# Two macaron half-steps around an attention block: tile 13's rows of the second half turned by transposing DMA, and the written-out order laid out anew

## The reference, cut to what matters

```
def ffn(x):                                   # 128 -> 512 -> 512 -> 512 -> 128, exact gelu
    h = silu(x @ w1.T * w1_s) * (x @ w2.T * w2_s)
    h = gelu(h @ h1.T * h1_s)
    h = gelu(h @ h2.T * h2_s)
    return h @ w3.T * w3_s

def attention(x):                             # per sequence of 256 tokens, no softmax matrix
    h = layer_norm(x) * gamma + beta
    keys, values = h @ Wk.T + bk, h @ Wv.T + bv
    w = exp((keys @ Wka.T + bka) / sqrt(128))
    w = w / cumsum(w, axis=1)
    return cumsum(w * keys, axis=1) * values

x = x + 0.5 * ffn(layernorm(x))               # x is 16 sequences x 256 tokens x 128 features
x = x + attention(layernorm(x))
x = x + 0.5 * ffn(layernorm(x))
```

## Time and profile before

| | |
|---|---|
| runs, median of 3 | 367.9 us (365.8 to 368.27) |
| the profiled execution's own time | 367.03 us |
| its span | 365.2 us |
| PE busy | 356.0 us, 97% |
| DVE busy | 309.7 us, 85% |
| ACT busy | 291.9 us, 80% |
| POOL busy | 174.5 us, 48% |
| granted TensorE clock | 1.0 |
| mean DMA rate | 67 GB/s |

### The profile page before, as it was taken

The page is one execution under the profiler, slowest core; times in us unless marked ns, Lnnn a source line. Parts: engine busy times, 40 slices in busy tenths (PEclk is TensorE's granted clock), DMA queues, the critical chain, the costliest instruction groups (busy, mean ns, idle before and its releaser), DMA issues.

```text
span 365.2 us, 5048 instructions
## 1 busy us (share of the span) xinstructions
PE 356.0 (97%) x1524; PEld 276.7 (76%) x1524; DVE 309.7 (85%) x542; ACT 291.9 (80%) x475; POOL 174.5 (48%) x271
## 2 busy tenths in 40 slices
PE   6899999999999999999999999999999999999996
PEld 1678888878777677887777778788778777868885
DVE  4989877898999989988998988998889899685733
ACT  4798777997997899779979888978876985757763
POOL 3476247388178398656556537352364342210000
PEclk9999999999999999999999999999999999999999
DMA  7725505134006003502113008030030030600001
GB/s 248 252 86 168 173 2 115 29 78 110 17 4 163 9 0 63 173 0 64 55 58 88 1 0 144 2 116 1 2 106 11 4 85 0 173 3 29 1 2 59
DMA packets 30206, 24.58 MB, mean 67 GB/s; under 512 B 20065, under 2 KB 21345, under 8 KB 29921
## 3 DMA queue, kind: packets, MB, share of 16 engines
q1 hardware_dynamic: 29312, 23.30, 23.8%
q10 hardware_dynamic: 864, 0.93, 0.8%
HBM read 18.89 MB, written 2.19 MB: 58 GB/s over the span
## 4 chain that ended last, share of the span: by engine, by line
PE 85%; ACT 4%; DVE 3%; DMA 3%; issue 2%; POOL 1%; POOLq 0%; SPq 0%; DVEq 0%; ACTq 0%
PE hid_ps L724 56%; PE y_ps L724 7%; PE gate_ps L724 7%; PE up_ps L724 6%; PE xt_ps L920 2%; PE xt_ps L917 2%; PE xt_ps L913 2%; DMA wide<-rows 1%; DMA raw_w<-w1t 1%; PE gate_ps L788 1%; ACT hid_ps L983 1%; DVE act_lo L1184 1%; PE up_ps L788 1%; DVE gate L1162 1%; ACT tanh L964 1%
## 5 line engine op out<-in xcount | busy, mean ns | idle before, releaser
L724 PE MATMUL hid_ps<-act_hi,hi_h 128*128 128x512 f32 (+1 forms) x368 | 148.4, 404 | 0.4 <-DVE act_lo L1184 0.4
L724 PE MATMUL hid_ps<-act_lo,hi_h 128*128 128x512 f32 (+1 forms) x368 | 143.4, 390 | 0.0
L983 ACT ACTIVATE hid_ps<-hid_ps,vec 128x512 f32<-128x512 f32 x104 | 68.5, 661 | 43.5 <-PE hid_ps L724 42.7
L1184 DVE TENSOR_TENSOR act_lo<-hid_ps,act_hi 128x512 fp32r<-128x512 f32 x104 | 70.0, 681 | 23.7 <-ACT act_hi L990 23.0
L724 PEld LDWEIGHTS hid_ps<-act_hi,hi_h 128*128 128x128 f32 x368 | 69.1, 188 | 21.4 <-DVE act_lo L1184 6.2
L724 PEld LDWEIGHTS hid_ps<-act_lo,hi_h 128*128 128x128 f32 x368 | 69.1, 188 | 16.9 <-issue 2.4
L990 ACT ACTIVATE act_hi<-hid_ps 128x512 fp32r<-128x512 f32 x104 | 61.3, 599 | 2.2
L1184 DVE TENSOR_TENSOR act_lo<-full,act_hi 128x512 fp32r<-128x512 f32 x53 | 38.7, 739 | 15.3 <-ACT act_hi L990 14.7
L724 PE MATMUL hid_ps<-act_hi_second,hi_h 128*128 128x512 f32 x128 | 51.4, 401 | 0.0
L724 PE MATMUL hid_ps<-act_lo_second,hi_h 128*128 128x512 f32 x128 | 50.0, 390 | 0.0
L641 POOL TENSOR_TENSOR xnt<-xt_sb,wide 128x512 f32<-128x512 f32 x22 | 28.8, 1307 | 39.1 <-DMA wide<-rows 31.0
(11 more groups left out here) (173 smaller groups left out, 598.5 us busy)
## 6 DMA issues: line engine op xcount, KB each, us to landing
wide<-rows SPq DMA_DIRECT2D x44, 256.0 KB, 3.9
out<-xt_sb SPq DMA_DIRECT2D x7, 256.0 KB, 4.2
raw_h<-h2t SPq DMA_DIRECT2D x4, 256.0 KB, 6.5
x_sb<-x SPq DMA_DIRECT2D x1, 1024.0 KB, 5.0
xt_sb<-xt SPq DMA_DIRECT2D x1, 1024.0 KB, 5.0
x_sb<-x SPq DMA_DIRECT2D x3, 256.0 KB, 3.5
raw_h<-h1t SPq DMA_DIRECT2D x2, 256.0 KB, 5.7
xt_sb<-xt SPq DMA_DIRECT2D x2, 256.0 KB, 4.1
```

What stands on the lines that cost most here:

```text
L724: mm = eng.matmul(ps, w, a, start=(first and n == 0), stop=(last and n == len(seq_) - 1))
L983: eng.activation(gelu_out(n, T, m)[:, :], home23(n, T, m)[:, :], ACT.Gelu, scale=col("sh1" if n == 2 else "sh2", m)).then_inc(s_gelu[n], 1)
L1184: eng.tensor_tensor(act_lo[a][:, m, :], full[:, :], act_hi[a][:, m, :].bitcast(F32), ALU.subtract).then_inc(s_lo[n], 1)
```

## The change

The tuple `BY_DMA` gets `("ffn", 13)`. The list of PE loses `13:u`; POOL gets `13:split`, SP `13:turn`, ACT `13:join`. Apart from these four items every engine's list holds the same items as before, in an order laid out anew. The parts of it that the prediction speaks of:

- Opening: ACT examines w2 before it converts w1; DVE takes tile 1's statistics after `low1.0` instead of between `gate.0` and `gate.1`; ACT does `tanh.2` after `high1.0` and `high1.1`.
- SP: `a7:turn` moves from directly behind `a6:turn` to behind the new `13:turn`, `8:store` and `9:store`; `10:store` ahead of `a7:park`, `11:store` ahead of `15:park`. Before, `9:store`, `10:store` and `11:store` stood between `15:park` and `15:wide`.
- POOL: `a7:split` moves from behind `a6:split` to behind the new `13:split`, which follows `a5:dt`.
- ACT: `a7:join` moves from behind `10:high2.2` to behind the new `13:join`, which stands between `11:high2.0` and `11:gelu2.1`.
- PE: `10:p4` moves from ahead of `11:p2.0` to behind `11:p2.1`; `12:p1.2` takes its place. DVE: `a5:pool` and `a5:values` move ahead of `11:low1.2`, `11:low1.3`, `10:low3.1` and `12:gate.0`.
- SP: `a6:turn` directly behind `12:turn`, ahead of `11:wide`; ACT: `a6:join` directly behind `12:join`.

```diff
 START
-        "hi:w1 bits:w2 hi:w2 z 0:t vec:s1",
-        "tanh.0 tanh.1 bits:h1.1 bits:h1.3 tanh.2 high1.0 high1.1 bits:h2.0 tanh.3 bits:w3 high1.2 z.0 z.1 "
+        "bits:w2 hi:w1 hi:w2 z 0:t vec:s1 0:tanh.0 0:tanh.1 bits:h1.1 bits:h1.3",
+        "high1.0 high1.1 tanh.2 tanh.3 bits:h2.0 bits:w3 high1.2 z.0 z.1 high1.3 bits:h2.3 1:t 0:gelu2.0 "
...
-        "stats aggr veps bits:w1 norm.0 norm.1 flag:copy1 norm.2 bits:h1.0 0:t bits:h1.2 vec:scales",
-        "gate.0 stats gate.1 up.0 flag:raise2 up.1 flag:copy2 low1.0 aggr gate.2 veps up.2 gate.3 bits:h2.1 "
+        "stats aggr veps bits:w1 norm.0 flag:copy1 norm.1 norm.2 bits:h1.0",
+        "t bits:h1.2 vec:scales gate.0 gate.1 up.0 flag:raise2 up.1 flag:copy2 low1.0 stats gate.2 aggr veps "
...
 STEPS, SP
-        "11:wide a6:turn a7:turn 12:park a6:park",
-        "12:wide a6:wide",
-        "",
-        "13:park a7:park 13:wide a7:wide",
-        "",
-        "park wide 8:store 15:park",
-        "9:store 10:store 11:store wide store",
+        "12:turn a6:turn 11:wide 12:park 12:wide a6:park a6:wide",
+        "13:turn 8:store 9:store a7:turn 13:park",
+        "",
+        "10:store a7:park",
+        "wide a7:wide 14:park 14:wide 11:store 15:park 15:wide",
...
+        "12:store 13:store store",
 STEPS, POOL
-        "10:xn.1 a5:xn.0 a5:xn.1 norm a4:weight a4:dt 12:split a6:split a7:split",
+        "a4:weight a4:dt 12:split a6:split",
+        "xn.0 xn.1 12:norm a6:norm a5:weight",
+        "xn.0 xn.1 a6:xn.0 a6:xn.1 a5:dt 13:split a7:split 13:norm a7:norm",
 STEPS, PE
-        "9:p4 10:p2.3 a5:values 10:p3.0 10:p3.1 12:p1.0 12:p1.1 10:p3.2 10:p3.3 a6:logits 10:p4 11:p2.0 13:u "
-        "11:p2.1 12:p1.2 11:p2.2 12:p1.3 11:p2.3 a6:keys",
+        "12:p1.0 12:p1.1 10:p3.2 10:p3.3 a6:logits 12:p1.2 11:p2.0 11:p2.1 10:p4 11:p2.2 12:p1.3 11:p2.3 "
+        "a6:keys",
 STEPS, ACT
+        "10:high3.3 a6:logits gelu2.0 high2.0 join a7:join gelu2.1 high2.1 gelu2.2 high2.2 tanh.2 high1.0 "
...
-BY_DMA = (("att", 1), ... ("ffn", 11), ("ffn", 12))
+BY_DMA = (("att", 1), ... ("ffn", 11), ("ffn", 12), ("ffn", 13))
```

More of the change, by code:

```diff
@@ L53 @@
     "SP": (
-        "park wide 3:park 3:wide a0:park a0:wide 4:park 4:wide a1:turn a1:park 5:park a1:wide 5:wide 6:park",
-        "",
-        "6:wide a2:turn a2:park 7:park a3:turn",
[12 rows of a table added]
         "",
@@ L59 @@
         "",
-        "a2:wide 7:wide turn 9:turn a3:park park a4:turn a3:wide wide 9:park 9:wide 10:turn a5:turn a4:park "
-        "a4:wide 10:park a5:park 10:wide 11:turn a5:wide 11:park 12:turn",
-        "11:wide a6:turn a7:turn 12:park a6:park",
-        "12:wide a6:wide",
-        "",
-        "13:park a7:park 13:wide a7:wide",
-        "",
-        "park wide 8:store 15:park",
-        "9:store 10:store 11:store wide store",
-        "store",
-        "store",
[1 row of a table added]
     ),
     "POOL": (
-        "norm hi:h2.0 hi:h2.1 hi:h2.2 hi:h2.3 hi:w3 xn.0 xn.1",
-        "",
[L75 to L78, removed]
[14 rows of a table added]
         "",
-        "split a4:split 8:norm a2:weight norm a3:xn.0 a3:xn.1 8:xn.0 8:xn.1 xn.0 a2:dt",
[1 row of a table added]
         "",
-        "10:split a5:split a4:norm 9:xn.1 a4:xn.0 10:norm a3:weight a4:xn.1 a5:norm a3:dt split 10:xn.0 "
-        "10:xn.1 a5:xn.0 a5:xn.1 norm a4:weight a4:dt 12:split a6:split a7:split",
[L84 to L90, removed]
[2 rows of a table added]
     ),
     "PE": (
[21 rows of a table removed]
[22 rows of a table added]
         "14:p1.2 13:p3.0 13:p3.1 14:p1.3 13:p3.2 13:p3.3 15:p1.0 15:p1.1 13:p4 14:p2.0 14:p2.1 14:p2.2 "
@@ L210 @@
 BY_PE = (0, 1)
-BY_DMA = (("att", 1), ("att", 2), ("att", 3), ("att", 4), ("att", 5), ("att", 6), ("att", 7), ("ffn", 8), ("ffn", 9), ("ffn", 10), ("ffn", 11), ("ffn", 12))
+BY_DMA = (("att", 1), ("att", 2), ("att", 3), ("att", 4), ("att", 5), ("att", 6), ("att", 7), ("ffn", 8), ("ffn", 9), ("ffn", 10), ("ffn", 11), ("ffn", 12), ("ffn", 13))
 AGGREGATE = 2
```

## The result

The changed kernel takes **369.63 us** (median of 6 runs, 368.93 to 370.23), the kernel before 367.02 us beside it (6 runs, 365.8 to 368.27): ratio 1.0072, 95% interval 1.0052 to 1.0093. It is 2.6 us slower. The profiled execution took 369.21 us, its span is 367.4.

The account below looks back on a forecast made before the run. PE, busy 97% of the span, was taken as the bound. Terms -0.5 - 1.0 + 0 + 0.3 + 0.6 + 0 summed to -0.6 us, giving 366.4 or 367.3 by base; forecast 366.7 us, range 364.0 to 369.5.

Parts of the forecast that it names:

- Tile 13's norm: DVE statistics wait for the join, 1.9 us later, delaying tile 13's first products on PE: +0.6 us, ends 0 and +1.5.
- 0.9 us that were missing: Tile 13's low part ready at 278.7 but wanted by PE at 277.8; about half, 0.4, was counted.
- my sign for a late turn: PE idle over 1 us between 255 and 285 would show that the a7 DMA turn lands late.
- The joins at 11:p2.3: Two joins on ACT delay 11:gelu2.1, so PE's 11:p2.3 starts later: +0.3 us, ends 0 and +1.5.
- the late-turn rival: a7:turn lands at 266.4, ACT's a7:join holds up 11:gelu2.1, PE loses some 3.1 us: 369.5 us; chance 0.2.
- Transposes: Tile 13's four transposes (13:u, 0.47 us in the chain at 260.74) leave PE: -0.5 us.
- Stores: Stores issued ahead of 15:park let tile 15's wide land sooner, recovering PE's 1.1 us near 322: -1.0, ends 0 and -1.1.
- My rival, that the landing is slow for another reason: Tile 15's broadcast was not slow from the stores, so PE's 1.1 us at 322 stay: 367.4 us; chance 0.15.
- Opening: Second layer starts sooner but PE waits for POOL's low part of block 2: 0, ends -0.75 and +0.3 us.
- My sign for an opening that goes through: A second layer whose low part of block 2 starts before 19 us would show the opening's gain goes through.
- Rest of the order: a6:turn and a6:join moves and dozens of ACT and DVE swaps: 0, ends -0.5 and +1.0 us.
- my sum of -0.6: All terms: -0.5 - 1.0 + 0 + 0.3 + 0.6 + 0 = -0.6 us on 367.03 us, giving 366.4.

Follow-up runs that it names:

- the kernel with 13 by DMA: Kernel before with only tile 13's rows turned by DMA (split, turn, join; a7's moved with them), stores, opening and other orders unchanged: 371.68 us, ratio 1.0145.

## Why the prediction was wrong

**Tile 13's norm: the failed step.** The step said that statistics come 1.9 us late and that "norm, park, wide and POOL's two passes follow at the same length, because `13:wide` stands behind `a7:park` in SP's list now as before". They did not. How late each link is, after against before (two of the rows of before: SP, then POOL):

```profile
268.47 0.42 SPq L560 DMA_DIRECT2D wide<-rows  x1
271.97 1.29 POOL L641 TENSOR_TENSOR xnt<-xt_sb,wide 128x512 f32<-128x512 f32 x1
```

| link | before | after | late |
|---|---|---|---|
| 13:stats starts | 261.38 | 263.82 | 2.44 |
| 13:park issued | 265.01 | 267.44 | 2.43 |
| 13:wide issued | 268.47 | 271.17 | 2.70 |
| POOL's first pass | 271.97 | 275.93 | 3.96 |
| ACT's high part | 274.94 | 279.39 | 4.45 |

The join began at 262.62, not 262.1, which is the half us in the first link. `13:wide` stands behind `a7:park` as before, and that adds 0.27. Then the broadcast: POOL's pass came 3.50 us after its issue before, 4.76 now (+1.26). Then the passes, 1.70 and 1.54 us for 1.29 and 1.27, with the gaps +0.49. Of the 4.45 us the slack took 2.2 (the high part was ready at 274.94 + 0.62 in the kernel before, PE came at 277.76), and the rest is PE's stop, 2.28. With the low part the term is 2.7, not 0.6, and over the end of 1.5 that I gave it. My slack was right, the lateness was not: 4.45 us where I had 1.9. I even took only half of the 0.9 us that were missing by it, since items between the links "can give way". None did; the links behind stretched instead. And I read the wait at `a7:park` as neutral since the kernel before has it too. There it was hidden; once the chain had no slack, the position had a price: 271.17 against 269.00 with the items swapped, 2.17 us. A stop of PE over 1 us between 255 and 285 was my sign for a late turn; it came, and stood for a late broadcast.

**The joins at 11:p2.3.** I had +0.3. PE starts `11:p2.3` at 266.82, 0.38 us after the product ahead of it where a slot is 0.23: 0.15 us late, too short to be listed as idle, and half of what I gave it. A turn takes 2.7 to 4.3 us in this trace, so the late-turn rival did not happen; its price, 369.5, is near the time measured, but by another mechanism.

**Transposes.** -0.5, as forecast: `8:p4` to `11:p4` is +2.37, which is 2.7 + 0.15 - 0.5.

**Stores.** -1.0 forecast, -1.07 from `11:p4` to `13:p4`; alone the move gives 0.6 in the trace and 1.1 in the medians. Right in place and about in size, but not by the mechanism that I gave. I took 1.5 us of landing to be the stores' doing; the landing shortened by 0.39 us (4.77 to 4.38), and the wide was issued 0.44 us sooner behind its park (1.64, 2.08 before). That the two together, 0.8 us, came near the 1.0 that I took is luck. My rival, that the landing is slow for another reason, was nearer to the truth on the landing and wrong on the gain.

**Opening.** 0 forecast (up to +0.3), +0.55 here. Counted from PE's first product, the second layer starts 0.73 us earlier and ends 0.51 earlier (24.91 and 23.89), so most of the gain lasted up to there, and PE's wait for POOL did not take it as I argued; `low1.2` moved up as well (17.04 from 17.88, 0.33 us counted from the first product). The step that failed is that I stopped there. Tile 2's broadcast comes earlier too, and with it POOL's pass, which in six of eight profiles falls into DVE's low parts of tile 0; by `0:p4` the gain is gone in two and more than gone in six. My sign for an opening that goes through, a low part of block 2 before 19 us, was met (18.39) and could not tell: with the opening of before put back, and as early a first product, it was 18.83.

**Rest of the order.** 0 forecast, ends -0.5 and +1.0; +0.69 up to `8:p4`, with the stop of 1.17 us at 138.17 and without that at 180.99. Inside the ends, on the bad side. Profiles of one order differ here by up to 1 us (181.2 to 182.1 us from `0:p4` to `8:p4` in four with the old order, 181.8 to 182.7 in ten with the new one), so the size is rough.

**The sum.** With 2.7 for tile 13, 0.15 for the joins, and 0.55 and 0.7 in place of the zeros, my sum of -0.6 becomes +2.6, against +2.69 in the traces.

Not settled: why the broadcast takes 4.7 us. It did in both profiles of the kernel after, with the opening back (4.70), and without the store between (POOL's pass came 4.9 us after its issue, 4.8 in the kernel after), but with only `4:dt` moved the pass came 3.4 us after it, issued at the same time. The runs of that kernel spread over 4.5 us, those with `13:wide` first over 1.6, which would fit a landing that differs from one execution to the next; one profile each can't show it. Part of the spread is the clock: three of its twelve executions had a mean granted clock of 0.995, and they took 370.05 to 371.48 us.

## What to carry to other kernels

A wait in SP's list of transfers, which are issued in order, costs nothing only while the transfer behind it has slack: when a change makes the producer later, walk the queue again and put the urgent transfer ahead of the one that waits for other work. Add up lateness link by link, and let no link "give way" unless a row shows its idle time. A stage that comes earlier moves its transfers too, so an opening is judged by a product 30 us behind it, not by its own end. Look at the granted clock of every execution, too: behind the same stop it fell in two profiles and not in two others, and by itself makes a run some 1.5 us longer.

## What the runs showed of the hardware

DVE and POOL stretched each other when POOL read from SBUF and DVE had both operands there. All instructions of DVE's line L1184 in the kernel after: with one operand in PSUM (`hid_ps`) none of 104 took over 693 ns, with both in SBUF (`full`) up to 2301 (ns min/median/max):

```profile
L1184 DVE TENSOR_TENSOR act_lo<-hid_ps,act_hi x104: 621/684/693, 41.4 to 327.1; 128x512 fp32r<-128x512 f32 x104
L1184 DVE TENSOR_TENSOR act_lo<-full,act_hi x53: 624/685/2301, 13.0 to 361.3; 128x512 fp32r<-128x512 f32 x53
```

In the kernel before, a low part with one operand in PSUM took its plain 0.69 us from 272.72 on, while POOL's pass ran (271.97 to 273.26). Where tile 13's passes ran, DVE's timeline of the kernel after has

```profile
275.80 0.68 DVE L1184 TENSOR_TENSOR act_lo<-full,act_hi 128x512 fp32r<-128x512 f32 x1
276.39 1.78 DVE L1254 TENSOR_TENSOR wgt_keys<-wgt,rcsum 128x512 f32<-128x512 f32 x1
```

POOL's pass from 275.93 took 0.4 longer than its usual 1.29, up to the end of DVE's low part at 276.48; DVE's next took 1.1 longer than its usual 0.68, up to about POOL's end at 277.63. So each was held for about as long as the other still ran. The Trainium skill (SBUF — State Buffer, Who interferes with whom) says that a DVE instruction with two SBUF inputs contends with a POOL instruction that reads SBUF; this trace agrees, in both directions.

The granted clock fell to 0.5 for some 3.4 us right behind a stop of PE of 2.1 us in two profiles (the second of the kernel after, and the one with the opening put back). It stayed at 1.0 behind the same stop in two others, and behind the longest, 3.23 us, in the kernel with 13 by DMA. Of the executions of kernels whose profile has a stop of 1.8 us or more, 14 of 37 had a mean granted clock of 0.995 or less; of those whose profile has none over 1.3 us, the kernel before among them, 11 of 146. That fits a stop that makes the fall likelier; no run tests it.
